# Eight PSUM banks in one free list, a new order of the projection blocks, and an output staging buffer in an attention and FFN layer

## The reference, cut to what matters

```
q = x @ q_w.T;  k = x @ k_w.T;  v = x @ v_w.T          # k, v: one head
scores = q k^T / sqrt(128), causal mask, softmax over keys
a = (softmax @ v) @ o_w.T
x1 = layernorm(x + a)
out = layernorm(x1 + (x1 @ (w * scale)^T + bias))
```

## Time and profile before

| | us |
|---|---|
| median of 2 timed runs | 2288.6 (2273.16 and 2304.04) |
| profiled execution | 2277.62 |
| its span on the slowest core | 2276.1 |
| spans of the 8 cores | 2270.1 to 2276.1 |

### The profile page before, as it was taken

The page is one execution under the profiler, slowest core; times in us unless marked ns, Lnnn a source line. Parts: engine busy times, 40 slices in busy tenths (PEclk is TensorE's granted clock), DMA queues, the critical chain, the costliest instruction groups (busy, mean ns, idle before and its releaser), DMA issues.

```text
span 2276.1 us, 26021 instructions; the slowest of 8 cores (2270.1 to 2276.1 us)
## 1 busy us (share of the span) xinstructions
PE 1535.5 (67%) x7216; PEld 671.1 (29%) x7216; DVE 904.9 (40%) x1985; ACT 907.0 (40%) x2270; POOL 374.3 (16%) x399
## 2 busy tenths in 40 slices
PE   0799962455555566666566666669989599779773
PEld 0344431222222222222233332333333233223221
DVE  0000002445555555555555555550436406405244
ACT  0112113655555565665555555551123213312421
POOL 0000020000000000000000000005655175265431
PEclk9999985666677577777577777679999899889986
DMA  9222289900000000000000000005643553463253
GB/s 140 46 38 37 39 100 111 111 11 1 1 1 1 1 1 1 1 1 1 1 1 1 1 1 1 1 1 151 169 134 111 162 162 104 149 170 106 83 167 92
DMA packets 43640, 137.06 MB, mean 60 GB/s; under 512 B 5835, under 2 KB 5868, under 8 KB 42988
## 3 DMA queue, kind: packets, MB, share of 16 engines
q1 hardware_dynamic: 28988, 84.02, 11.9%
q0 software_dynamic: 5296, 34.60, 11.8%
q10 hardware_dynamic: 9216, 16.78, 2.8%
HBM read 153.21 MB, written 33.55 MB: 82 GB/s over the span
## 4 chain that ended last, share of the span: by engine, by line
PE 43%; DVE 16%; ACT 15%; issue 14%; DMA 7%; another core or an unknown queue 3%; POOL 1%; DVEq 1%; ACTq 0%; SPq 0%; POOLq 0%
ACT expS L395 12%; PE psT L259 10%; DVE mpart L374 8%; PE psO L479 7%; PE psT L828 5%; DMA wost<-wo_bf 4%; PE psT L762 3%; PE psU L828 2%; PE psO L828 2%; PE psS L346 2%; PE psU L762 2%; DMA trib_s<-tri 2%; PE psS L439 2%; DVE ycs L721 2%
## 5 line engine op out<-in xcount | busy, mean ns | idle before, releaser
L374 DVE TENSOR_REDUCE mpart<-psS 128x1 f32<-128x512 f32 (+3 forms) x367 | 205.9, 598 | 374.5 <-PE psS L355 370.2
L479 PE MATMUL psO<-expST,Vsb 128*128 128x512 bf16 x640 | 259.8, 552 | 94.1 <-ACT expST L463 87.5
L395 ACT ACTIVATE expS<-psS,negm 128x512 bf16<-128x512 f32 (+3 forms) x367 | 224.8, 618 | 225.3 <-DVE negm L378 224.6
L789 POOL TENSOR_TENSOR ycs<-yscr,xres 128x512 f32<-128x512 f32 x64 | 82.6, 1290 | 1360.8 <-ACT yscr L778 1244.5
L439 PE MATMUL psS<-diagP,expS 128*128 128x128 bf16 x1250 | 150.7, 263 | 147.8 <-ACT expS L395 111.1
L259 PE MATMUL psT<-xTbf,qwst 128*128 128x512 bf16 x1024 | 221.2, 379 | 0.2 <-ACT Vsb L241 0.2
L346 PE MATMUL psS<-KT,QTO 128*128 128x512 bf16 (+3 forms) x367 | 157.7, 477 | 63.6 <-ACT expS L395 38.7
L407 DVE TENSOR_REDUCE den<-dpart 128x1 f32<-128x2 f32 (+2 forms) x192 | 29.9, 156 | 414.9 <-ACT expS L395 414.9
L439 PEld LDWEIGHTS psS<-diagP,expS 128*128 128x128 bf16 x1250 | 103.7, 118 | 194.6 <-issue 190.9
L416 ACT ACTIVATE diagP<-ident_s,rcp 128x128 bf16<-128x128 bf16 x256 | 102.7, 401 | 144.4 <-DVE rcp L412 144.4
L395 ACT ACTIVATE expS<-psT,negm 128x512 bf16<-128x512 f32 (+3 forms) x185 | 114.6, 624 | 104.5 <-DVE negm L378 103.8
(11 more groups left out here) (91 smaller groups left out, 2242.7 us busy)
## 6 DMA issues: line engine op xcount, KB each, us to landing
wost<-wo_bf SPq DMA_DIRECT2D x64, 512.0 KB, 4.6
fwst<-fw_bf SPq DMA_DIRECT2D x64, 512.0 KB, 3.3
xres<-xT ACTq DMA_DIRECT2D x64, 256.0 KB, 4.7
outT<-ycs SPq DMA_DIRECT2D x64, 256.0 KB, 3.5
xTbf<-xT POOLq DMA_DIRECT2D x1, 8192.0 KB, 61.1
qwst<-qw POOLq DMA_DIRECT2D x16, 512.0 KB, 5.8
wo_bf<-wo POOLq DMA_DIRECT2D x4, 2048.0 KB, 80.4
fw_bf<-fw POOLq DMA_DIRECT2D x4, 2048.0 KB, 99.0
```

The lines of the kernel that those rows point to most:

```text
L374: mc=mcol + kc: e.reduce_max(mpart[:, mc:mc + 1], slot[:, 0:wdt], axis=AX.X),
L395: e.activation(expS8[:, (par * 4 + qt % 4) * S + kc * W: (par * 4 + qt % 4) * S + kc * W + wdt], slot[:, 0:wdt], AF.Exp, bias=negm8[:, nco ...
L479: base=base: e.matmul(psO[:], Vsb[:, kt * 128:(kt + 1) * 128], expST2[:, base + kt * W: base + (kt + 1) * W], start=(kt == 0), stop=(kt == ...
L789: pbuf=pbuf: e.tensor_tensor(pbuf[:, ot * W:(ot + 1) * W], yscr[:, (ot % 3) * W:(ot % 3) * W + W], xres[:, (ot % 3) * W:(ot % 3) * W + W], ...
```

## The change

In attention the ring of seven and the separate `psO` become one free list of eight banks. A user takes the bank at the head; it goes to the end of the list where its move out is emitted. `av_unit` takes a bank at j = 0, holds it until j = c, and waits for that bank's last move out in place of that of `psO`. In stage C:

- the blocks run O0, O1, F0, F1, O2, O3, F2, F3;
- `emit_out` writes into a new buffer `outb` of three slots, from which the store reads; the first VectorE operation of tile ot waits for the store of tile ot-3 to have landed; each slot has its own counter;
- a residual add waits for the VectorE read of its own tile of chunk c-2, not for the stores;
- to make room, `yscr` and `zscr` have two slots and `castsc` 14 in place of 16 (OROT 5 to 4, OD 4 to 3), and part 0 of an O tail has three statistics pairs for four;
- the first broadcast waits for the last copy out of its bank, whichever kind it was.

```diff
-                    s = ring_i[0] % 7
-                    ring_i[0] += 1
+                    s, sev = ring_free.popleft()
...
-                    ring_ev[s] = E_ex
+                    ring_free.append((s, E_ex))
...
                 if pj == 0:
-                    w0 = list(E_trevall[par]) + [E_msd[par], oev[0]]
+                    s, sev = ring_free.popleft()
+                    av_slot[par] = s
+                    w0 = (list(E_trevall[par])
+                          + [E_msd[par], sev])
...
+                    ring_free.append((s, oev[0]))
...
-                OROT, OD = 5, 4
+                OROT, OD = 4, 3
...
                     for ot in ots:
-                        em = p.op("vector", lambda e, ot=ot, pbuf=pbuf:
-                                  e.tensor_tensor(
-                            pbuf[:, ot * W:(ot + 1) * W],
+                        sl = ot % 3
+                        wom = [E_abc2[c], E_castF[c][ot], E_sqF[c][ot]]
+                        if odc[sl] > 0:
+                            wom.append(("od%d" % sl, 16 * odc[sl]))
+                        E_outm[c][ot] = p.op("vector", lambda e, ot=ot,
+                                             pbuf=pbuf: e.tensor_tensor(
+                            outb[:, (ot % 3) * W:(ot % 3 + 1) * W],
                             pbuf[:, ot * W:(ot + 1) * W], abc2_s[:],
...
+                            in_=outb[:, (ot % 3) * W:(ot % 3 + 1) * W]),
+                            waits=[E_outa[c][ot]], inc="od%d" % sl)
+                        odc[sl] += 1
...
-                        if ot >= 3:
-                            w = w + [E_addO[c][ot - 3]]
+                        if ot >= 2:
+                            w = w + [E_addO[c][ot - 2]]
...
                     if c >= 2:
-                        wadd.append(("od", 256 * (c - 1)))
+                        wadd.append(E_outm[c - 2][ot])
...
-                blocks = [("O", 0), ("O", 1), ("F", 0), ("O", 2),
-                          ("F", 1), ("O", 3), ("F", 2), ("F", 3)]
+                blocks = [("O", 0), ("O", 1), ("F", 0), ("F", 1),
+                          ("O", 2), ("O", 3), ("F", 2), ("F", 3)]
```

More of the change, by code:

```diff
@@ L487, in av_unit @@
                 if pj == c:
-                    oev[0] = p.op("scalar", lambda e, h=h, c=c: e.copy(
-                        QTO[:, h * S + c * W: h * S + c * W + W], psO[:]),
-                        waits=[E_av], inc="a")
+                    oev[0] = p.op("scalar", lambda e, bk=bk, h=h, c=c: e.copy(
+                        QTO[:, h * S + c * W: h * S + c * W + W],
+                        bk[:, 0:W]), waits=[E_av], inc="a")
+                    ring_free.append((s, oev[0]))
             for c in range(NCH):
@@ L573, in build_program @@
                 E_x1b = [[None] * NT for _ in range(NCH)]
+                E_outm = [[None] * NT for _ in range(NCH)]
+                odc = [0, 0, 0]
                 E_x1t = [[None] * NT for _ in range(NCH)]
@@ L655, in emit_bcast_a @@
                     Eb = (E_lnbO if kind == "O" else E_lnbF)[c]
[L656 to L660, removed]
+                    w = [Eb, last_abc[0] if last_abc[0] else E_attn_done]
                     p.op("tensor", lambda e, rp=rp: e.matmul(
@@ L732, in emit_out @@
[L732 to L736, removed]
+                        sl = ot % 3
[5 more added lines that the diff above has]
+                            outb[:, (ot % 3) * W:(ot % 3 + 1) * W],
+                            pbuf[:, ot * W:(ot + 1) * W], abc2_s[:],
+                            AluOpType.mult), waits=wom, inc="v")
@@ L737, in emit_out @@
+                        E_outa[c][ot] = p.op("vector", lambda e, ot=ot:
+                                             e.tensor_tensor(
+                            outb[:, (ot % 3) * W:(ot % 3 + 1) * W],
+                            outb[:, (ot % 3) * W:(ot % 3 + 1) * W],
+                            bbc2_s[:],
+                            AluOpType.add), waits=[E_outm[c][ot]], inc="v")
+                        p.op("sync", lambda e, c=c, ot=ot: e.dma_start(
                             out=out_h[ot * 128:(ot + 1) * 128,
@@ L951, in build_program @@
                     pend[k]()
-                p.op("gpsimd",
-                     lambda e: e.wait_ge(sems["od"], 16 * NT * NCH))
+                p.op("gpsimd", lambda e: (
+                    e.wait_ge(sems["od0"], 16 * odc[0]),
+                    e.wait_ge(sems["od1"], 16 * odc[1]),
+                    e.wait_ge(sems["od2"], 16 * odc[2]))[-1])
         nc._prog = p
```

67 lines of the change are left out of this document (31 added, 36 removed), and 1 row of the table SEMS.

## The result

The changed kernel takes 2287.9 us (median of 43 runs, 2279.2 to 2384.1) against 2278.4 us for the kernel before in the same rounds (42 runs). The ratio is 1.0042, with a 95% interval of 1.0031 to 1.0054: 9.6 us slower by the ratio, inside 2%, and still resolved. I had forecast 2277 us, 0.6 us under the kernel before, and no change. In some executions the cores of one die run at a lower granted clock and the time is some per cent longer (the 2304.04 ahead of the prediction stands apart like one of these); the ratios, and all times in the sections behind this one, leave such executions out.

What follows compares the result with a forecast made beforehand. Waits bound the kernel: VectorE and ScalarE taking turns in attention, and in stage C adds waiting for stores. Order -6.3, slots +7.7, bank -2 gave -0.6 on 2277.6, so 2277 us; 8 in 10 from 2248 to 2308.

Steps and rivals of the forecast that it cites:

- Attention: Attention stage: VectorE and ScalarE take turns and set the period, so the eighth bank brings only -2 us, range -28 to 0.
- The stall: Stage C, O2 and O3: GpSimd's residual adds wait for all stores of chunk c-2; O2 101.3 to 92.4, O3 101.4 to 80.5 us.
- The order's -6.3 us: Stage C, new block order: O3 -20.9, F0 +7.5, F1 +16.0, O2 -8.9, summing to -6.3 us.
- The slots of `outb`: Output tiles in stage C: VectorE waits for the store of tile ot-3; together +7.7 us, range 0 to +39.
- my formula: Output tiles: a slot's round is 1.71 us plus the landing, shared by three slots; a 4.4 us landing gives 2.04 a tile.
- the +3.4 it allows: Output blocks: with 4.4 us landings, up to +3.4 us on the 12 tiles ahead of the last delayed weight load.
- The port decides in O2: Rival, stage C: VectorE's output tiles beside GpSimd take 2.47 us, not 1.76; +8.5, 2286 us; chance 0.14.
- the pace of the first norm: O2's outputs beside GpSimd's adds: 16 tiles of the first norm, beside a busy GpSimd, took 2.47 us each; alone 1.43.
- The slots turn the sign: Rival, `outb` in stage C: landings as long as the longest seen, +39 for +7.7; 2308 us, slower than before; chance 0.06.
- Stores no longer hold up the weights: Rival, F1, O2 and F3: outputs leave the path, three times 16.7 us and 5.5 of slot waits; 2221 us; chance 0.06.
- The bank pays: Rival, attention: a spare bank lets TensorE run ahead wherever VectorE waits for it; -28 for -2, 2251 us; chance 0.13.
- The stall stays: Rival, stage C: something else holds O2 and O3 at 101 us, so 8.9 and 20.9 are lost; 2307 us; chance 0.07.

Runs made afterwards that it cites:

- The bank alone: The kernel before with the free list of eight banks in attention and nothing else; ratio 1.0005 (0.9992 to 1.0019).
- the repeat: Changed kernel, changed kernel with outputs stored in place, and kernel before with only the new block order, rerun side by side on another chip: 1.0043, 1.0028, 1.0011.
- Order alone: The kernel before with the new block order and the changed wait of the first broadcast, stores still from `ycs`; ratio 1.0009 (0.9976 to 1.0042).
- the in-place kernel: The changed kernel with outputs made and stored in place in `ycs`, without `outb` and its slot waits; ratio 0.9992 (0.9979 to 1.0005).
- two slots: The changed kernel with two slots in `outb` in place of three; 2319.6 us, ratio 1.0193 (1.0175 to 1.0211).
- the runs with moved loads: Weight loads of groups 2 to 15 issued by ScalarE, not SP: changed kernel 0.9844; kernel before 0.9962; kernel before with new order, stores in place, 0.9810.

## Why the prediction was wrong, step by step

**Attention: right on where the time is set, 2 us too much given.** VectorE waits 414.3 us for exponentials, 414.9 before, and the stage differs by 1 us. The bank alone gives a ratio of 1.0005. On this round between VectorE and ScalarE a spare bank for TensorE brought nothing.

**The stall: right.** O2 and O3 lost their wait for stores and came down to 95.6 and 77.2 us; the rival in which something else holds them falls.

**The order's -6.3 us: the first step that failed.** Each of its four blocks was right to 4 us (F1 to 5.5 in the repeat). Order alone against before, in means of the cores: F0 +7.6 (forecast +7.5), F1 +19.7 (+16.0), O2 -9.7 (-8.9), O3 -24.2 (-20.9). Sum -6.6; in the repeat -5.1. But that is against the one long execution of the kernel before. The kernel with the bank alone has the same stage C, and its profile gives a second value: 730.2 us for the stage beside 731.5, against 725.0 and 728.2 with the new order, so -4.3 in the mean. The timed runs show -3.4 and +0.2 us in the mean over the cores. And on the slowest core, which is the metric, the order won nothing that holds: +2.0 and +2.5 us by the ratios (-3.4 and +1.8 by the medians), and -6.3 us (0.9972) lies just outside both intervals. So a net gain of 6 us, put together from four terms of 8 to 25 us that were each read from one core of one execution, was not there. What it is worth in the mean, between -3.4 and 0, stays open.

**The slots of `outb`: the second step, right in kind and 1 to 3 us too cheap.** The mechanism is shown: the in-place kernel takes the time back, two slots make it grow. I had +7.7 us; measured were 10.3 in the profiles, 9.1 in the timed means over the cores and 10.7 on the slowest core. By phase:

| | forecast | measured (mean of two pairs of profiles) |
|---|---|---|
| F1 | +1.5 | +4.8 |
| O2 | +2.5 | +1.9 |
| F3 | +1.5 | +3.7 |
| tail | +2.2 | -0.1 |

For core 4 my formula gave the pace right: with a landing of 4.4 us, its median in F1, it says 2.04 us a tile, and F1 took 1.97. I then took 1.5 of the +3.4 it allows, with the argument that "slower tiles leave the stores more time". That counts the slack twice: the 1.76 us of F3 was already the slower tile, and without slots the tiles of F1 took 1.65. And a median landing hides the single long ones: cores 0 to 3 had median landings of 3.2 us in F1, for which the formula gives 1.64 a tile and no wait, and they waited 2.1 to 2.5 us all the same. The sum of the single waits (5.5 us in F1, 5.3 in F3, 2.9 in O2 on core 4) fits the longer stretch of the stores, 5.1 us in F1, better than the mean slack of a tile does. In the tail the error goes the other way. I took landings of 3.1 us. That was core 1; on the other seven cores of the same execution the medians are 2.4 to 2.7 us. After, on core 4:

```profile
DMA to landing us min/median/max: 2.4/2.5/2.6
```

With 2.5 us the formula gives (1.71 + 2.5) / 3 = 1.40 us a tile, under the 1.43 that VectorE needs, and this core doesn't wait there (the longest total in the tail is 1.5 us, on core 2).

**One core for eight: a term I never set.** I worked on one core and never asked whether all would pay alike. They don't. The waits on the slots, in the trace after, on core 1 and on core 6:

```profile
DVE outb L733 <- DMA outT<-outb: 7.6, 12, 1.2
```

```profile
DVE outb L733 <- DMA outT<-outb: 22.2, 16, 2.9
```

Core 1 is the fastest core after (2269.5 us), core 6 is among the slowest (2284.1); core 4, the slowest, waited 13.7 us. In the repeat the cores line up better. Its fastest core (core 3, 2264.9 us) and its slowest (core 7, 2289.6 us):

```profile
DVE outb L733 <- DMA outT<-outb: 9.3, 12, 1.2
```

```profile
DVE outb L733 <- DMA outT<-outb: 23.2, 21, 2.8
```

There the stores of F1 landed after 5.3 us in the median on core 7, after 3.3 on core 3, and F1 took 107.4 and 101.1 us. In place, where no one waits for a landing, core 7 took 96.7 for F1 in its repeat. What makes the landings of some cores longer, no run shows.

The slots are not all of the spread. In the timed runs the slowest core's span is 8.0 us over the mean of the cores after, 11.4 in the repeat; 4.8 to 6.6 before; but 9.3 and 7.3 with the order alone and 6.8 and 8.6 in place, where there are no slot waits.

**The sum.** Forecast -6.3 + 7.7 - 2 = -0.6. In the mean over the cores the runs give -3.4 to +0.2 for the order, +9.1 for the slots (repeats) and nothing that shows for the bank, so +6 to +9. The changed kernel's mean was 2278.6 in the repeats, 9.5 us above 2269.1, and 2277.3 in the runs of the result above, 7 to 8 us over what the kernel before takes on the three chips. On the slowest core there was more of it in the repeats, 15.5 us (2275.6 to 2291.1). The sign came from three terms that I had all set on the fast side, the order's 6 first, then the 1 to 3 missing from the slots and the bank's 2. That the forecast of 2277 still lay within 0.5% of the result says little for it: terms of up to 25 us each way had to cancel.

**The rivals.** *The port decides in O2* named 2286 us, within 2 us of the result, and that is luck: its condition, 2.47 us a tile in O2, did not occur. In place the sixteen stores of O2 take 26.1 us in the mean over the cores, 1.63 a tile, and with the slots 31.1, 1.94 a tile. So my reading that the outputs beside the adds would go at the pace of the first norm was wrong too. *The slots turn the sign* had the right mechanism, at 10 us and not at its 39, which needed landings of 5.7 us throughout; I had nothing between 7.7 and 39. *Stores no longer hold up the weights* did not occur, and the runs with moved loads show about what it would have been worth: I had 2221 us for it, and 2242.7 were reached with `outb` and 2233.3 in place. *The bank pays* and *The stall stays* fell with the bank alone and with O2 and O3.

## What to carry to other kernels

When a store takes over the place where another engine used to wait, ask what stands behind the new waiter in every list; here VectorE's wait of 1 to 2 us went through SP's list to the weight loads and so to TensorE. Loads that the bottleneck needs don't belong behind stores that wait for an engine: moving them was worth 10 to 21 us for each block with outputs where nothing else held it (12 to 18 in the kernel without `outb`), and only then did the better block order pay. Before adding a buffer to break a wait, see whether the new order has already made the wait free; and for a metric that is the slowest of eight cores, read a landing time on all eight cores before pricing a wait with it, and price the wait by the core on which it is longest. A net term of a few us made of large ones of both signs needs more than one execution to be believed.

## What the runs showed of the hardware

VectorE's output operations took longer in the kernels in which GpSimd works beside them. The groups of output operations after (mean ns of one behind the busy time), then that of the first of the two operations in the kernel with the new order, stores in place and moved loads:

```profile
L733 DVE TENSOR_TENSOR outb<-ycs,abc_s 128x512 f32<-128x512 f32 x64 | 49.9, 780 | 15.2 <-DMA outT<-outb 13.7 <-DVE bbc_s L691 0.9 <-POOL castsc L810 0.6
L738 DVE TENSOR_TENSOR outb<-outb,bbc_s 128x512 f32<-128x512 f32 x64 | 53.7, 839 | 6.7
```

```profile
L719 DVE TENSOR_TENSOR ycs<-ycs,abc_s 128x512 f32<-128x512 f32 x64 | 64.6, 1009 | 0.7 <-DVE bbc_s L681 0.5 <-POOL ycs L788 0.2
```

The kernel before had 734 and 726 ns for the two. GpSimd was busy for 8.28 of 28.2 us in the output phase of F3 before, and for 22.80 of 40 us from 1800 to 1840 us in the last of these kernels. The Trainium skill (SBUF — State Buffer, SBUF: two separate sides) has the two engines share one pair of ports. The trace agrees in kind: 1009 ns against 734, 37% more on an operation with both inputs in SBUF, averaged over phases with and without GpSimd's work and on two different cores. What this costs in the kernel's time, no run here separates; with moved loads the slower outputs at least hold up no weight load.
